# Transposing the short probability rests of two narrow units in one group, on one Trainium2 core

## The reference

```python
def _L1_xattn_ref(x, cond, wq, wk, wv, wo, norm_w):
    xn = rmsnorm(x, norm_w)
    q = (xn @ wq).reshape(B, T, N_HEADS, HEAD_DIM)
    k = (cond @ wk).reshape(B, S, N_KV_HEADS, HEAD_DIM)
    v = (cond @ wv).reshape(B, S, N_KV_HEADS, HEAD_DIM)
    qg = q.reshape(B, T, N_KV_HEADS, n_rep, HEAD_DIM)
    scores = jnp.einsum('btgrd,bsgd->bgrts', qg, k) * scale
    attn = jax.nn.softmax(scores.astype(jnp.float32), axis=-1).astype(q.dtype)
    out = jnp.einsum('bgrts,bsgd->btgrd', attn, v).reshape(B, T, N_HEADS * HEAD_DIM)
    return residual + out @ wo
```

## Time and profile before

| what | value |
|---|---|
| median of 3 executions | 2058.31 us |
| the profiled execution | 2059.61 us |
| its span, first to last instruction | 2057.8 us |
| TensorE busy | 2021.4 us (98%) |
| VectorE busy | 1440.6 us (70%) |
| ScalarE / GpSimd busy | 965.3 us (47%) / 649.6 us (32%) |
| granted TensorE clock, share of full speed | 0.998 |

### The profile page before, as it was taken

The page is one execution under the profiler, slowest core; times in us unless marked ns, Lnnn a source line. Parts: engine busy times, 40 slices in busy tenths (PEclk is TensorE's granted clock), DMA queues, the critical chain, the costliest instruction groups (busy, mean ns, idle before and its releaser), DMA issues.

```text
span 2057.8 us, 31311 instructions
## 1 busy us (share of the span) xinstructions
PE 2021.4 (98%) x11482; PEld 1758.8 (85%) x11482; DVE 1440.6 (70%) x2472; ACT 965.3 (47%) x1814; POOL 649.6 (32%) x534
## 2 busy tenths in 40 slices
PE   8999999999999999999999999999999999999998
PEld 8999988888888887788888888888888877888887
DVE  5322367777777767888888677777677777888886
ACT  3222354444444444555555444444444444555553
POOL 1000043222222254454444432222222354444441
PEclk9999999999999999999999999999999999999999
DMA  7789742222222222333333332222222223333322
GB/s 207 169 175 206 189 93 64 67 71 72 58 67 72 80 63 73 98 106 103 88 99 95 104 89 71 71 56 66 72 73 59 64 86 85 79 88 91 88 72 84
DMA packets 262538, 191.02 MB, mean 93 GB/s; under 512 B 197522, under 2 KB 199986, under 8 KB 259826
## 3 DMA queue, kind: packets, MB, share of 16 engines
q1 hardware_dynamic: 262386, 189.03, 35.3%
HBM read 132.66 MB, written 56.26 MB: 92 GB/s over the span
## 4 chain that ended last, share of the span: by engine, by line
PE 91%; DVE 5%; ACT 1%; POOL 1%; issue 1%; DMA 1%; SPq 0%; DVEq 0%; ACTq 0%; POOLq 0%
PE acc_bank L887 11%; PE q_bank L845 9%; PE q_bank L847 8%; PE q_bank L849 8%; PE acc_bank L269 8%; PE acc_bank L271 8%; PE acc_bank L270 8%; PE t_bank L867 7%; PE ctx_bank L269 4%; PE ctx_bank L270 4%; PE ctx_bank L271 4%; PE s_bank L808 2%; PE s_bank L269 2%; PE s_bank L805 2%; PE s_bank L811 2%; PE s_bank L270 2%
## 5 line engine op out<-in xcount | busy, mean ns | idle before, releaser
L1324 POOL TENSOR_TENSOR prob<-prob,rinv 128x1232 f32<-128x1232 f32 x128 | 288.3, 2252 | 1002.5 <-DVE rinv L1208 1002.5
L1166 DVE TENSOR_REDUCE mx<-s_bank 128x4 f32<-128x308 f32 x512 | 243.1, 475 | 204.0 <-PE s_bank L811 154.3
L1066 ACT ACTIVATE q_s<-q_bank 128x512 fp32r<-128x512 f32 x192 | 114.7, 597 | 494.0 <-PE q_bank L849 490.9
L887 PE MATMUL acc_bank<-pT_s,vals_s 128*128 128x512 f32 x1024 | 338.8, 416 | 0.0
L845 PE MATMUL q_bank<-x_s,w_s 128*128 128x512 f32 x768 | 318.9, 415 | 0.0
L849 PE MATMUL q_bank<-x_s,w_s 128*128 128x512 f32 x768 | 313.2, 408 | 0.0
L847 PE MATMUL q_bank<-x_s,w_s 128*128 128x512 f32 x768 | 312.4, 407 | 0.0
L269 PE MATMUL acc_bank<-o_s,w_s 128*128 128x512 f32 x752 | 305.2, 406 | 5.9 <-DVE o_s L1199 5.9
L271 PE MATMUL acc_bank<-o_s,w_s 128*128 128x512 f32 x752 | 294.4, 392 | 0.0
L270 PE MATMUL acc_bank<-o_s,w_s 128*128 128x512 f32 x752 | 293.5, 390 | 0.0
L1057 ACT ACTIVATE prob<-prob,rstd 128x308 f32<-128x308 f32 x256 | 141.0, 553 | 265.8 <-DVE prob L1170 239.1
(11 more groups left out here) (107 smaller groups left out, 4032.5 us busy)
## 6 DMA issues: line engine op xcount, KB each, us to landing
stream<-x_back SPq DMA_DIRECT2D x128, 256.0 KB, 2.7
x_front<-stream SPq DMA_DIRECT2D x96, 256.0 KB, 3.4
x_back<-stream SPq DMA_DIRECT2D x96, 256.0 KB, 3.7
kvw_raw<-kvw SPq DMA_DIRECT2D x17, 1024.0 KB, 8.6
k_scr<-k_out SPq DMA_DIRECT2D x36, 308.0 KB, 9.7
keys_s<-k_scr SPq DMA_DIRECT2D x128, 77.0 KB, 2.4
v_scr<-v_out SPq DMA_DIRECT2D x8, 1024.0 KB
vals_s<-v_scr SPq DMA_DIRECT2D x512, 6.5 KB
```

What stands on the lines that cost most here:

```text
L887: mm = pe.matmul(out, w, pT_s[:, part], start=i == mine[0] and part == 2 * n and w is v[0], stop=i == mine[-1] and w is terms[-1][0] and p ...
L1166: dve.tensor_reduce(top, scored, AX_X, ALU.max).then_inc(s_max, 1)
L1324: pool.tensor_tensor(view, view, rinv[:, slot].unsqueeze(2).broadcast_to([P, TILES * GH, CTX]), ALU.mult).then_inc(p_norm, 1)
```

## The change

The rests of two narrow units (an even unit and the odd one behind it) are copied beside each other by GpSimd, 64 columns each, and transposed in one group of four, where there were two groups of four with 64 columns each. That group stands in the even step (s - 1 is the odd unit), behind the second half of the queries and ahead of the even unit's second block of values. The two value matmuls of the even unit's short block go behind the step's first projection, or, where there is none in that place (units 32, 34, 96, 98: `carried`), into the next step, behind the first half of its queries. The even unit's `split_o` and `rest_o` move into the next step, the latter behind its tile 1 (tile 3 where carried). VectorE takes the pair's two rests ahead of the next unit's queries. Counts of finished items (`acc_mm`) go by a new order, `ended`, and groups by a new numbering, `plan.t`. The core of the diff:

```diff
+    def split_values(self, u):
+        return 0 <= u < NU and kind(u).name == "B" and u % 2 == 0
+    def carried(self, u):
+        return self.split_values(u) and (self.ahead(u + 2) or not self.projections(u + 2))
+    def turns(self, u):
+        return (0, 1, TWICE) if kind(u).name == "A" else (0, TWICE, 1) if u % 2 else (0, 1)
+    def rest_turn(self, u):
+        return self.t[(u if kind(u).name == "A" else u | 1, TWICE)]
...
         # load_vals(u)
-                    sp.wait_ge(acc_mm, plan.acc[("pv", u - 2, kind(u - 2).Q - 1)] + 1)
+                    sp.wait_ge(acc_mm, plan.ended[("pv", u - 2, kind(u - 2).Q - 1)])
...
         # turn(u, n)
-                after(pe, t_lo, 3 * u + n - 1)
+                after(pe, t_lo, item - 1)
+                if n == TWICE:
+                    pe.wait_ge(p_gathered, u + 1)
+                    p = rest[:, t] if n == TWICE else prob[:, u % 2, t, base:base + P]
...
         # TensorE, a narrow step
                     run(q, half)
+                    if plan.carried(s - 3):
+                        run(v_before, 2)
                     run(scores(s, 2), 1)
                     run(scores(s, 3), 1)
...
                     run(v, 3)
                     turned(0)
                     run(q, half)
-                    run(v, 9)
-                    turned(1)
+                    late_turns = plan.turns(s - 1)[1:]
+                    if behind:
+                        turned(late_turns[0])
+                        run(v, 3)
+                    else:
+                        run(v, 9)
+                        turned(late_turns[0])
                     if plan.stats_at(s) is not None:
                         stats(plan.stats_at(s))
-                    turned(2)
-                    if not plan.ahead(s):
-                        for gb, m in plan.projections(s):
-                            project(gb, m)
+                    for n in late_turns[1:]:
+                        turned(n)
+                    if behind and not plan.carried(s - 2):
+                        projected(projections[:1])
+                        run(v, 2)
+                        projected(projections[1:])
+                    else:
+                        projected(projections)
...
         # ScalarE, split_t of the pair: 64 rows to the same 64 rows, twice
+                        row = 64 * m if kind(u).name == "B" else 0
+                        e = act.activation(pT_s[row:row + 64, 2 * n + m], t_bank[item % 2][64 * m:64 * m + 64, :],
         # ScalarE, start of a step
+                if plan.split_values(s - 3) and not plan.carried(s - 3):
+                    split_o(s - 3, 0)
...
         # VectorE, tile_scores and rest_t
                 if t == 0 and u >= 2:
-                    dve.wait_ge(t_mm, 3 * (u - 2) + 3)
+                    dve.wait_ge(t_mm, plan.prob_read(u - 2))
+                    dve.wait_ge(p_gathered, u - 1)
                 dve.wait_ge(s_max, TILES * u + t + 1)
...
+                        rows, hi, lo = (REST_A, 0, 64) if kind(u).name == "A" else (64, 64 * m, 64 - 64 * m)
+                        e = dve.tensor_tensor(pT_s[lo:lo + rows, 2 * n + m], t_bank[item % 2][64 * m:64 * m + rows, :],
+                                              pT_s[hi:hi + rows, 2 * n + m].bitcast(F32), ALU.subtract)
...
         # VectorE, a narrow step
+                    for t in range(TILES):
+                        if s < NU:
                             tile_scores(s, t)
+                        if t == (3 if plan.carried(s - 3) else 1) and plan.split_values(s - 3):
+                            rest_o(s - 3, 0)
...
+                    rest_early = plan.split_values(s - 2)
+                    if rest_early:
+                        turned(TWICE)
                     next(q, None)
                     next(q, None)
...
         # GpSimd, normalise(u)
+                pool.wait_ge(p_norm, u + 1)
+                if u:
+                    pool.wait_ge(t_mm, plan.rest_read_before(u))
+                else:
+                    pool.tensor_copy(rest[:, :, 64 * slot:64 * slot + 64], prob[:, slot, :, SC - REST_B:SC])\
+                        .then_inc(p_gathered, 1)
```

More of the change, by code:

```diff
@@ L143, in __init__ @@
             projections = [("proj", gb, m) for gb, m in self.projections(s)]
[L144 to L149, removed]
+            values = [("pv", s - 2, m) for m in range(kind(s - 2).Q)] if 0 <= s - 2 < NU else []
+            acc += projections + values if self.ahead(s) else values + projections
+            first = len(projections) if self.ahead(s) else 1 if self.split_values(s - 2) else 0
+            if self.carried(s - 3):
+                ends.append(("pv", s - 3, 0))
+            now = [] if self.carried(s - 2) else values
+            ends += projections[:first] + now + projections[first:]
+            turns += [(s - 1, n) for n in self.turns(s - 1)]
         self.q = {item: n for n, item in enumerate(queries)}
         self.acc = {item: n for n, item in enumerate(acc)}
+        self.ended = {item: n + 1 for n, item in enumerate(ends)}
+        self.t = {item: n for n, item in enumerate(turns)}
         self.q_splits = {item: n for n, item in enumerate(i for i in queries if i[0] == "q")}
@@ L157, in late @@
         found = self.projections(s) if s >= 0 else []
-        return found[-1:] if s < NU and kind(s).name == "B" and not self.ahead(s) else []
+        return found[-1:] if not self.ahead(s) and (s < NU and kind(s).name == "B" or self.split_values(s - 2)) else []
     def ahead(self, s):
@@ L721, in load_vals @@
                     col = w * h % P
+                    if kind(u).name == "B" and blk == TWICE and u % 2:
+                        row = (row + 64) % P
                     sp.dma_start(vals[row:row + t1 - t0, blk, 0:last - first, col:col + w], src)\
@@ L785, in _ @@
                         store(gb, m)
+                if s == NU + 1:
+                    for gb, m in plan.late(NU):
+                        load_back(gb + 1, m)
             for m in range(XC):
@@ L954, in _, with projected @@
             run(queries(0), 24)
+            v = iter(())
             for s in range(STEPS):
                 q = queries(s + 1) if s + 1 < NU else iter(())
-                v = values(s - 2) if 0 <= s - 2 < NU else iter(())
+                v_before, v = v, values(s - 2) if 0 <= s - 2 < NU else iter(())
                 a = s < NU and kind(s).name == "A"
                 def turned(n):
-                    if 0 <= s - 1 < NU:
+                    if n in plan.turns(s - 1):
                         turn(s - 1, n)
+                def projected(now):
+                    for gb, m in now:
+                        project(gb, m)
+                projections = plan.projections(s)
+                behind = plan.split_values(s - 2)
                 if a and s < 2:
@@ L990, in _ @@
                     if plan.ahead(s):
-                        for gb, m in plan.projections(s):
-                            project(gb, m)
+                        projected(projections)
+                        projections = []
                     run(v, 3)
@@ L1259, in _ @@
                     if s >= 1 and not plan.rest_later(s - 1):
-                        rest_t(s - 1, TWICE)
+                        for n in late_turns[1:]:
+                            turned(n)
                     for gb, m in plan.projections(s):
-                        add_result(gb, m)
+                        if (gb, m) not in plan.late(s):
+                            add_result(gb, m)
                     if plan.stats_at(s) is not None:
@@ L1265, in _ @@
                 else:
-                    if s < NU:
-                        for t in range(TILES):
+                    for t in range(TILES):
+                        if s < NU:
                             tile_scores(s, t)
+                        if t == (3 if plan.carried(s - 3) else 1) and plan.split_values(s - 3):
+                            rest_o(s - 3, 0)
                     for gb, m in plan.late(s - 1):
```

116 lines of the change are left out of this document (59 added, 57 removed).

## The result

The changed kernel took 2070.61 us (median of 6 executions, 2066.46 to 2073.35); the kernel before, run beside it, 2058.83 us (6 executions, 2057.96 to 2060.08). The ratio is 1.0055, 95% interval 1.0044 to 1.0066: slower by 11.8 us, where 2.1 were forecast, and above the range.

What follows compares the result with a forecast made beforehand. TensorE's instruction stream, busy 98% of the span, was taken as the bound, VectorE in steps 35 and 36. Terms: -11.0 + 4.1 + 2.4 + 1.0 + 1.0 + 4.6 = +2.1 us, giving 2060.4 us, range 2051 to 2067.

Steps and rivals of the forecast that it cites:

- the values' wait in odd steps: Odd unit's values wait for `rest_o`, now behind tile 1 of the same step: 24 x 0.17 = +4.1 us.
- The rival by which these holes don't open: Odd steps: `rest_o` is read in time and TensorE keeps the whole 0.44 us; 2051.9 us, chance 0.24.
- The second term: Steps with s % 4 == 1: tenth projection matmul starts 0.20 us late behind the slipped rest; 12 x 0.20 = +2.4 us.
- The third term: Even steps: VectorE's pair ahead of the queries exposes 0.04 us before the next first score; 25 x 0.04 = +1.0 us.
- the other rival: Even steps: queries come late, so 25 steps lose 0.3 us at the next first score; 2066.9 us, chance 0.26.
- The third wait on tile 0: Added wait (`p_gathered`) on tile 0 of every unit: 0.02 us in 48 plain narrow steps, +1.0 us.
- the zone's waits: Steps 34 to 38 and twins: queries' rest behind the pair, carried matmuls ahead of scores; 2 x 2.3 = +4.6 us.
- Step 33 (and 97) waits for VectorE ahead of its projection in any case: Steps 33 and 97: removing the four transposes there gains nothing, counted at 0.
- 64 I leave at 0 (0 to +1): Step 64, the one wide step taken as changed: cost 0, between 0 and +1 us.
- waits until an even step's end, and the keys and x queued behind wait for the next step's scores anyway: SP's queue: the later `load_vals` delays nothing, as vals are used two steps on; no cost.

Runs made afterwards that it cites:

- the late order: Changed kernel with VectorE splitting the pair's rest behind the next unit's queries in steps 34, 36, 98 and 100 alone: 2059.32 us, ratio 1.0002.
- the filled kernel: Changed kernel with useless identity transposes in TensorE's long waits at steps 33, 34, 36 and 97, 98, 100: 2061.78 us, ratio 1.0011.
- The two combined kernels: Weights loaded first, waits filled in 30 and 94; one has units 32-35, 96-99 unpaired, other VectorE's pair late there, 33 and 97 filled: 2053.04, 2053.03 us.

## Why the prediction was wrong, point by point

**Right: the plain steps.** The sum gave odd steps 10.65 and 10.40 and even ones 10.5; they are 10.70, 10.43 to 10.45, and 10.48 to 10.5. Both layers together gain 2.5, and step 63 0.5 (0.44 forecast): 3.0 against 11.0 - 4.1 - 2.4 - 1.0 - 1.0 = 2.5. Of the single terms, the values' wait in odd steps was the largest that the trace of before could not show. It is there in step 55 of the kernel after, VectorE and TensorE:

```profile
1053.91 0.68 DVE L1257 TENSOR_TENSOR o_s<-acc_bank,o_s 128x512 fp32r<-128x512 f32 x1
```

```profile
1054.43 0.30 PE L297 MATMUL s_bank<-keys_s,q_s 128*128 128x308 f32 x1
1054.69 0.94 PE L916 MATMUL acc_bank<-pT_s,vals_s 128*128 128x512 f32 x3
```

The rest ends at 1054.59 and the values start 0.10 behind it, at 1054.69 instead of 1054.57, and their three take 0.94 instead of 0.86: 0.20 in all, where 0.17 was written. The rival by which these holes don't open (odd steps of 10.04) is out. The second term is there too: in step 57 the rest ends at 1082.14, the tenth projection matmul starts 0.06 behind it, and the next follows after 0.33; it costs some 0.16 where 0.20 was written. The third term was 0.04 a step and is 0.01 to 0.03: the queries' rest is in time, so the other rival is out as well. The third wait on tile 0 costs 0.03, not 0.02 (the subtraction follows its maximum after 0.61, 0.58 before).

**Right in size: the zone's waits.** 2.3 us a layer were forecast and 2.2 measured with the clock at 1.00. The cause given (the queries behind the pair) is the one that the late order takes away. I had put the queries' end at 837.3, 15.1 us into step 34; in the filled kernel step 35's first score comes 15.3 us into it. The way from there to the sum is less right than the sum: the prediction had step 36 some 0.8 us late, and its first score is 1.6 late, that of step 37 3.2, that of step 38 2.2. That 2.3 was so close is in part luck.

**Wrong, and the main step that failed: "Step 33 (and 97) waits for VectorE ahead of its projection in any case", counted at 0, and the zone's waits priced at their own length.** Both take a wait of TensorE as worth its length. The wait of step 33 is indeed met at the same place, 9.5 us into the step, with the group and without it. But the longer wait was followed by a low stretch of clock, which costs 1.5 to 1.6 us where TensorE is full behind it: 3.3 us for steps 33 and 97, 4.2 us in steps 98 to 101 of the profiled execution. The filled kernel puts the whole at 8.8 us by the medians, of which 1.3 is step 65 in the profiles, that happened to have its transfer in time there. The material for this stood in the trace of before: steps 30 and 94 have a wait of 2.67 us and the granted clock of 0.50 behind it. The page gave 0.998 as the mean, and I read it as nothing; it is two stretches of 3.4 us.

**Wrong: "64 I leave at 0 (0 to +1)" and SP's `load_vals` "waits until an even step's end, and the keys and x queued behind wait for the next step's scores anyway".** The list of what is queued behind had keys and x; in steps 64 and 65 it has a quarter of the weights too, which nothing but the queue holds back. Step 64 itself is 0.1 us longer, step 65 1.5 us.

**Left open.** Why the ten loads of values in step 65 take 7.40 us to issue in one profile and 6.25 in another. Why a given wait is followed by the low clock in one execution and not in the next: steps 30 and 94 have a wait of 2.7 us in every kernel without filling, and the stretch behind it was there in step 94 in the kernel before and not in that after. The 1.3 us ahead of step 0 are such a stretch too, in code that the change leaves alone: behind a wait of 2.52 us that ends at 36.26 (2.30 before, and no low clock behind it). I did not try whether a longer filler at those places, or fewer transposes in it, does the same.

## What to carry to other kernels

Price a wait of the bounding engine as its length plus what comes behind it: look in the trace of before at the granted clock just behind each of its longest waits. Where an edit removes work that filled such a wait, the removal can cost more than the work did, and useless transposes into a free bank are a cheap cure. When an operation moves, read the whole queue behind its consumers for each kind of step, the rare ones too, and let an order that pays in 50 steps have an exception in the 4 where the bounding engine changes.

## What the runs showed of the hardware

- TensorE's clock fell to 0.50 for about 3.4 us behind waits of 2.04 to 3.17 us in a stream that is 98% busy, and in these profiles never behind those of 1.56 to 1.66 us. It didn't fall behind every longer one: in the kernel after, steps 35 and 37 start behind waits of 2.39 and 3.17 us with the clock at 1.00. Each such stretch cost 1.5 to 1.6 us (steps 30, 33, 94 and 97 with and without it: 21.4 and 19.9, 16.7 and 15.1). The Trainium skill (TensorE: Matmul & The Clock Gate, What's actually happening) says that a block of the chip sets the clock by how busy the array has been, in a beat of its own that does not start with the kernel. The traces agree as far as the stretch comes behind idle time, and behind the same wait in one execution and not in another.
- The spread of the times goes with the clock. The two combined kernels, with every wait over 2 us in the steps filled or gone, lie within 0.3 and 0.5 us (5 executions each), all at a mean clock of 1.000; the kernel after lies within 6.9 (6), the kernel before within 4.6 (15, beside those two), the fastest of them at 0.999 and the slowest at 0.996. The kernel before with only steps 30 and 94 filled lies within 1.8 (11).
- Sixteen transposes left 0.33 of the 2.04 us of wait in step 33, 0.43 us for four, and didn't hold up what follows: the step is 15.10 us long with them, as before the change.
